# The order of a chunk of the test-time-training scan on four engines, rearranged with the same operations

## The chip, the cores and the metric

One core of a Trainium2 chip runs the whole kernel. The metric is the device time of the execution in microseconds.

## What is computed

The kernel is one transformer block with adaptive layer norm on x of 4x1024x128. Its first half is what the change touches: a small two-layer network is trained by one gradient step for each of the 1024 time steps (on the 4 sequences of the batch), and the trained network is then applied to all tokens. Cut to what matters:

```python
def _mlp(params, h):
    W1, b1, W2, b2 = params
    return silu(h @ W1 + b1) @ W2 + b2
k, v = split(x @ W_KV)                    # time first: (1024, 4, 128) each
def step(params, kvt):
    g = grad(lambda p, k_t, v_t: mean((_mlp(p, k_t) - v_t) ** 2))(params, *kvt)
    return tuple(p - LR * gp for p, gp in zip(params, g)), None
params, _ = scan(step, (W1, b1, W2, b2), (k, v))
out = _mlp(params, x @ W_Q)
```

The second half is a mixture of eight experts with two active and one shared expert. The change leaves it as it is.

## The kernel before

The program is a row of blocks; in each, the engines run their own lists of instructions and meet by semaphores. The scan is one block. It goes through the 1024 steps in 32 chunks of 32 steps, so that a chunk is a tile of 128 columns (32 steps of 4 sequences). Within a chunk the steps depend on each other through the weights; the kernel solves this by iteration. It computes an estimate of the chunk from the weights at its start, with masked gram matrices (`mk`, `mk2`: only earlier steps count) that carry the effect of the steps before, and repeats it with the last estimate.

Three chunks are in work at a time. Chunk n+2 is prepared (names with `q_`: the projection to `kv`, its transpose `kvrow`, its gram matrices `GX`). Chunk n+1 gets a cheap estimate in bf16 (names with `l_` or a final L: `aL`, `eL`, `gL`), before the weights of its start are known exactly. Chunk n gets the f32 iterations (`h_`, a final H: `aH`, `e1H`, `e2H`, `e3H`), and from their result `ge` the weights W1b and W2p are updated. `W2pL` is W2p in bf16, brought forward by the cheap estimate's own sums, with which that of the next chunk is made.

The order is written out by hand. Each of TensorE, ScalarE, VectorE and GpSimd has a function `turn(n, r)` that lists its steps with `do(step, chunk, ring slot)`. Each step is a small function with its waits and one or two instructions. Turns -2 to 3 and 28 to 33 are unrolled, the others stand in a loop of four turns. An engine runs its instructions in the order of its list, and what it waits for holds up all that stands behind.

The steps that matter in what follows, with the lines of the profile:

- TensorE (L389 is the helper `mm`): `h_y_first` (the product aH,W2p) waits for the new W2p; `l_y_first` (W2pL,aL) for the new W2pL; `h_f_last` (W2p,e3H) for e3H; `h_sums1`, `h_sums2` (ge,kvrow and arowH,ge) for ge. `h_gram_a` is the gram product of aH, `h_y_old` a bf16 product with erowL and GaL. `l_turn_q0` (L437) transposes qL.
- VectorE (L770 is the helper `stt`): `l_mask_a1` writes GaL, `h_mask_e2` Ge2H (L845), `h_less1` nH (L853), `l_e_last` eL, `h_slope1` qH from tH and nH, `h_e_last` e3H, `l_mask_e` GeL, `h_g_last` ge, `h_new_W2` W2p, `l_new_W2` W2pL.
- The check of convergence runs beside: GpSimd's `chk_diff` (L993) writes `diff`, the difference between the last two estimates `ge` of a chunk. VectorE's `square` (L773) adds up the squares of `diff` (`chk_add_diff_g`, `chk_add_diff_e`) and of `ge` (`chk_add_norm_g`, `chk_add_norm_e`) into `sums`, each with an instruction that reads the sum out. After the scan these decide whether a slow exact path has to run. It does not with these inputs.
- GpSimd, chunk n+1: `l_less1` nL (L966), `l_more1` oL (L970), `l_slope1` qL (L974); then `q_shift` vb (L946) and `q_lower` GXb (L950).

Of the kernel before, what the change touches and what calls it, by code (L numbers as in the profile page):

```python
# [43 lines left out]
def program(nc, x, w_q, w_kv, w1, b1, w2, b2, w_router,  # L44
            s_w1t, s_b1, s_w2t, s_b2, cond, w_mod, slabs, ident_in, before_in, lower_in, tabs_in, xs, ys, out):
    with ExitStack() as ctx:
# [310 lines left out]
        with block() as blk:  # L357
# [29 lines left out]
            def _(pe):  # L387
# [200 lines left out]
                def turn(n, r):  # L588
                    do(h_gram_a, n, r)
                    do(h_y_old, n, r)  # L590
# [10 lines left out]
                    do(l_turn_q0, n + 1, r + 1)  # L601
                    do(q_turn, n + 2, r + 2)
                    do(h_turn_q0, n, r)
                    do(l_f_first, n + 1, r + 1)
                    do(h_f_add0, n, r)
                    do(h_f_first, n, r)
                    do(l_z_add, n + 1, r + 1)
                    do(l_turn_e2, n + 1, r + 1)
                    do(h_z_new, n, r)
                    do(h_turn_e2, n, r)  # L610
                    do(h_z_last, n, r)
                    do(l_gram_a1, n + 1, r + 1)
                    do(l_turn_a, n + 1, r + 1)
                    do(h_gram_e2, n, r)
# [5 lines left out]
                    do(q_grams, n + 2, r + 2)  # L620
                    do(l_gram_e, n + 1, r + 1)
                    do(h_f_add1, n, r)
                    do(h_turn_q1, n, r)
                    do(h_f_last, n, r)
                    do(l_turn_e, n + 1, r + 1)
                    do(h_turn_e3, n, r)
                    do(l_turn_q1, n + 1, r + 1)
                    do(l_f_second, n + 1, r + 1)
                    do(h_z_base, n + 1, r + 1)
# [6 lines left out]
                    do(l_sums, n + 1, r + 1)  # L636

# [10 lines left out]
            def _(act):  # L648
# [39 lines left out]
                def l_row_e(c, r):  # L688
                    nc.scalar.copy(erowL[1][:, :], LCb[:, 3 * P:4 * P]).then_inc(l_er2, 1)

                def h_act0(c, r):
                    act.wait_ge(h_z, 2 * c + 1)
                    nc.scalar.activation(aH[0][:, :], HZ[:, 0:P], ACT.Silu, bias=W1b[:, (r - 1) % 2, P:P + 1]).then_inc(h_a, 1)  # L693

                def h_tanh0(c, r):
                    nc.scalar.activation(tH[0][:, :], HZ[:, 0:P], ACT.Tanh, bias=b1n[(r - 1) % 2][:, 0:1], scale=-0.5).then_inc(h_t, 1)
# [37 lines left out]
                def turn(n, r):  # L734
                    do(l_act0, n + 1, r + 1)
# [4 lines left out]
                    do(l_row_q0, n + 1, r + 1)  # L740
                    do(h_row_q0, n, r)
                    do(q_rows, n + 2, r + 2)
                    do(l_act1, n + 1, r + 1)
                    do(l_row_e2, n + 1, r + 1)
                    do(h_row_e2, n, r)
# [1041 lines left out]
```

## Time and profile before

| | us |
|---|---|
| median of 3 runs | 749.01 (747.5 to 749.43) |
| the profiled execution, its time | 740.31 |
| its span | 738.5 |
| busy in it: TensorE | 581.0 |
| VectorE | 449.1 |
| GpSimd | 347.2 |
| ScalarE | 322.1 |

The page gives busy times over the whole span. A line of the timeline gives the start of an instruction in us from the span's start, its length, its engine, its line and what it writes and reads. Lengths are from start to result; the next instruction of an engine may start before that. PE stands for TensorE's products, PEld for its weight loads, DVE for VectorE, ACT for ScalarE, POOL for GpSimd. An f32 product of 128 columns is two passes (x2).

### The profile page before, as it was taken

The page shows a single profiled execution, that of the slowest core. Times are in us where ns is not written, and L with a number is a line of the kernel's source. Part 1 is how long each engine was busy: PE and PEld are TensorE (multiplying, and loading weights), DVE is VectorE, ACT ScalarE, POOL GpSimd, SP SyncE. Part 2 cuts the span into 40 slices and gives each one's busy share as a digit, 9 for nine tenths or more (in the row PEclk, how much of TensorE's full clock was granted, in tenths as well). Part 3 has the DMA queues.
Part 4 walks back from the last instruction along what each step waited for, and adds up shares of the span by engine and source line. Part 5 has one row for each costly group of instructions (what it writes and reads, how often), then busy time and mean ns, then how long its engine had stood idle before and what let it go on. Part 6 is the DMA issues. An engine that isn't in the chain of part 4 may idle for free. (4 is left out here: it accounts for less than half of the span.)

```text
span 738.5 us, 14829 instructions
## 1 busy us (share of the span) xinstructions
PE 581.0 (79%) x4319; PEld 520.2 (70%) x4319; DVE 449.1 (61%) x1732; ACT 322.1 (44%) x1022; POOL 347.2 (47%) x558
## 2 busy tenths in 40 slices
PE   1459999999999999997739253003998999999937
PEld 1339999999999999996429252002997999999923
DVE  2847888888888888887286650100995444444505
ACT  1546666666666666663322041000674444434400
POOL 1035666666666666663730077774001555455430
PEclk9999999999999999999775575555899999999969
DMA  9069700000000000000000051111002777777648
GB/s 201 0 273 412 315 2 2 0 0 0 0 0 0 0 0 0 0 1 2 1 1 0 1 204 51 55 51 41 23 1 68 207 228 232 229 232 215 195 143 227
DMA packets 42879, 66.76 MB, mean 90 GB/s; under 512 B 7536, under 2 KB 30832, under 8 KB 42832
## 3 DMA queue, kind: packets, MB, share of 16 engines
q1 hardware_dynamic: 32048, 52.74, 22.8%
q0 software_dynamic: 4544, 9.45, 3.6%
q10 hardware_dynamic: 6240, 4.00, 2.0%
q8 instruction: 22, 0.36, 0.2%
q14 instruction: 25, 0.20, 0.1%
HBM read 36.25 MB, written 29.92 MB: 90 GB/s over the span
## 5 line engine op out<-in xcount | busy, mean ns | idle before, releaser
L1740 POOL DMA_INDIRECT ys<-yo,dst x78 | 74.8, 960 | 128.0 <-DVE yo L1698 112.0
L1621 ACT ACTIVATE hid<-bank,slab 128x256 f32<-128x256 f32 x156 | 63.7, 471 | 81.9 <-PE bank L1550 69.6
L1732 POOL DMA_INDIRECT xs<-hrow,slot_i x64 | 62.6, 979 | 66.6 <-POOLq L1271 47.4
L1561 PEld LDWEIGHTS bank<-slab,hid 128*128 128x128 f32 x624 | 75.6, 192 | 2.0
L1561 PE MATMUL bank<-slab,hid 128*128 128x128 f32 x624 | 75.8, 275 | 0.0
L1550 PE MATMUL bank<-hg,slab 128*128 128x256 f32 x312 | 74.0, 380 | 0.8 <-DVE hg L1674 0.5
L1550 PEld LDWEIGHTS bank<-hg,slab 128*128 128x128 f32 x312 | 56.2, 190 | 7.3 <-issue 0.7
L1533 PE MATMUL bank<-ident,yT 128*128 128x128 f32 x32 | 7.3, 313 | 55.4 <-issue 43.7
L1533 PEld LDWEIGHTS bank<-ident,yT 128*128 128x128 f32 x32 | 4.0, 156 | 57.2 <-issue 44.1
L1606 ACT ACTIVATE hx<-bank,sb 128x256 f32<-128x256 f32 x64 | 26.4, 473 | 40.2 <-remote 31.9
L389 PE MATMUL bank<-aH,W2p 128*128 128x128 f32 x192 | 42.1, 301 | 0.1
L389 PE MATMUL bank<-kv,W1b 128*128 128x128 f32 x192 | 41.2, 297 | 0.0
L1681 DVE SCALAR_TENSOR_TENSOR row<-xt,etab 128x2 f32<-128x2 f32 x39 | 8.6, 221 | 52.1 <-DMA ys<-yo,dst 52.1
L966 POOL TENSOR_TENSOR nL<-aL,ones 128x128 f32<-128x128 bf16 x32 | 17.7, 553 | 41.5 <-ACT aL L675 41.5
L1657 DVE CAST hhH<-hx 128x512 fp32r<-128x512 f32 x32 | 13.5, 423 | 36.8 <-ACT hx L1606 27.3
L978 POOL TENSOR_TENSOR nH<-aH,ones 128x128 f32<-128x128 f32 x32 | 14.6, 456 | 36.7 <-ACT aH L693 36.7
L389 PEld LDWEIGHTS bank<-aH,W2p 128*128 128x128 f32 x192 | 28.9, 190 | 3.3 <-DVE W2p L770 0.3
L1514 PE MATMUL bank<-hgH,w1H 128*128 128x256 f32 x64 | 20.8, 325 | 12.8 <-DVE hgL L1649 9.6
L389 PE MATMUL bank<-GX,ge 128*128 128x128 f32 x128 | 30.7, 322 | 0.1
L1649 DVE TENSOR_TENSOR hgL<-hT,hgH 128x256 fp32r<-128x256 f32 x16 | 6.7, 424 | 39.4 <-issue 37.1
L1613 ACT ACTIVATE yT<-bank,bs2T 128x256 f32<-128x256 f32 x16 | 7.6, 475 | 52.3 <-issue 34.9
L1693 DVE TENSOR_TENSOR yb<-bank,slab 128x256 f32<-128x256 f32 x39 | 16.6, 425 | 22.0 <-PE bank L1561 12.3
(322 smaller groups left out, 2039.1 us busy)
## 6 DMA issues: line engine op xcount, KB each, us to landing
slab<-in_slabs_dram SPq DMA_DIRECT2D x39, 578.0 KB
xs<-fill SPq DMA_DIRECT2D x34, 528.0 KB, 6.1
xt<-xs SPq DMA_DIRECT2D x39, 132.0 KB
xr<-in_L_attn_x_dram SPq DMA_DIRECT2D x8, 256.0 KB, 9.0
yg<-ys SPq DMA_DIRECT2D x4, 512.0 KB, 8.7
yg<-ys ACTq DMA_DIRECT2D x4, 512.0 KB, 9.6
ys<-yo,dst POOLq DMA_INDIRECT x78
xs<-hrow,slot_i POOLq DMA_INDIRECT x64
```

What stands on the lines that cost most here:

```text
L389: return pe.matmul(dst, lhs, rhs, start=start, stop=stop, skip_group_check=True)
L966: pool.tensor_tensor(nL[1][:, :], aL[1][:, :], ones2[:, 0:P], ALU.subtract).then_inc(l_n, 1)
L978: pool.tensor_tensor(nH[0][:, :], aH[0][:, :], ones2[:, 0:P], ALU.subtract).then_inc(h_n, 1)
L1514: mm = pe.matmul(u_half(t, n), w[:, n, :], h[t % 2][:, :], start=(m == 0), stop=(m == 2))
L1550: mm = pe.matmul(e_half(j, n), slab[j % RW][:, n * P:(n + 1) * P], hg[j % 2][:, :], start=True, stop=True)
L1561: mm = pe.matmul(bank[4 + j % 2][:, s * D:(s + 1) * D], hid[j % 2][:, n, s * P:(s + 1) * P], slab[j % RW][:, F + n * P:F + (n + 1) * P], s ...
L1606: nc.scalar.activation(hx[a][:, n % HALF, :], u_half(t, n), ACT.Gelu_apprx_tanh, bias=sb1[:, n:n + 1]).then_inc(x_ready, 1)
L1621: nc.scalar.activation(hid[j % 2][:, n, :], e_half(j, n), ACT.Gelu_apprx_tanh, bias=slab[j % RW][:, 2 * F + n:2 * F + n + 1]).then_inc(e_x, 1)
L1657: dve.tensor_copy(hi, hx[a][:, :, :]).then_inc(hi_ready, 1)
L1693: dve.tensor_tensor(yb[j % 2][:, :, :], bank[4 + j % 2][:, 0:SUB * D].rearrange("p (s d) -> p s d", s=SUB), slab[j % RW][:, 2 * F + FT:SLA ...
L1732: pool.indirect_dma_start(out=xs[:, :], out_offset=bass.IndirectOffsetOnAxis(ap=slot_i[:, c, k:k + 1], axis=0), in_=hrow[:, c, :], in_offs ...
L1740: pool.indirect_dma_start(out=ys[:, :], out_offset=bass.IndirectOffsetOnAxis(ap=dst[r][:, s:s + 1], axis=0), in_=yo[r][:, s, :], in_offset ...
```

## The change

The four lists `turn` are put in another order, and the waits that the new order makes needless or necessary are taken out or put in. No operation is added or taken away. On TensorE some of the bf16 products (`l_` steps and `h_y_old`) are moved next to each other. On ScalarE the tanh for aH comes ahead of its silu. On VectorE and GpSimd the parts of the check of convergence are moved.

```diff
--- before.py
+++ after.py
@@ -586,8 +586,6 @@
                     mm(HU[:, P:2 * P + 1], ge[r % 2][1][:, 1, :], arowH[1][:, :], True, True).then_inc(h_U2, 1)
 
                 def turn(n, r):
-                    do(h_gram_a, n, r)
-                    do(h_y_old, n, r)
                     do(h_y_first, n, r)
                     do(h_turn_a0, n, r)
                     do(l_gram_a0, n + 1, r + 1)
@@ -599,33 +597,33 @@
                     do(l_y_second, n + 1, r + 1)
                     do(h_y_second, n, r)
                     do(l_turn_q0, n + 1, r + 1)
+                    do(h_f_add0, n, r)
+                    do(l_f_first, n + 1, r + 1)
+                    do(l_turn_e2, n + 1, r + 1)
+                    do(h_turn_q0, n, r)
+                    do(h_f_first, n, r)
+                    do(h_turn_e2, n, r)
+                    do(l_z_add, n + 1, r + 1)
                     do(q_turn, n + 2, r + 2)
-                    do(h_turn_q0, n, r)
-                    do(l_f_first, n + 1, r + 1)
-                    do(h_f_add0, n, r)
-                    do(h_f_first, n, r)
-                    do(l_z_add, n + 1, r + 1)
-                    do(l_turn_e2, n + 1, r + 1)
                     do(h_z_new, n, r)
-                    do(h_turn_e2, n, r)
                     do(h_z_last, n, r)
                     do(l_gram_a1, n + 1, r + 1)
+                    do(h_gram_e2, n, r)
                     do(l_turn_a, n + 1, r + 1)
-                    do(h_gram_e2, n, r)
                     do(h_y_lag, n, r)
                     do(l_y_base, n + 1, r + 1)
                     do(l_y_add, n + 1, r + 1)
                     do(h_y_last, n, r)
                     do(h_turn_a1, n, r)
                     do(q_grams, n + 2, r + 2)
+                    do(h_f_add1, n, r)
                     do(l_gram_e, n + 1, r + 1)
-                    do(h_f_add1, n, r)
                     do(h_turn_q1, n, r)
                     do(h_f_last, n, r)
-                    do(l_turn_e, n + 1, r + 1)
                     do(h_turn_e3, n, r)
                     do(l_turn_q1, n + 1, r + 1)
                     do(l_f_second, n + 1, r + 1)
+                    do(l_turn_e, n + 1, r + 1)
                     do(h_z_base, n + 1, r + 1)
                     do(h_sums1, n, r)
                     do(h_z_cross, n + 1, r + 1)
@@ -634,6 +632,8 @@
                     do(l_z_base, n + 2, r + 2)
                     do(l_z_cross, n + 2, r + 2)
                     do(l_sums, n + 1, r + 1)
+                    do(h_y_old, n + 1, r + 1)
+                    do(h_gram_a, n + 1, r + 1)
 
                 pe.wait_ge(cleared, 5)
                 for n in range(-2, RING):
@@ -686,13 +686,14 @@
                     nc.scalar.copy(qrowL[1][:, :], LTb[:, 2 * P:3 * P]).then_inc(l_qr, 1)
 
                 def l_row_e(c, r):
+                    act.wait_ge(l_T2, 2 * c + 2)
                     nc.scalar.copy(erowL[1][:, :], LCb[:, 3 * P:4 * P]).then_inc(l_er2, 1)
 
                 def h_act0(c, r):
+                    nc.scalar.activation(aH[0][:, :], HZ[:, 0:P], ACT.Silu, bias=W1b[:, (r - 1) % 2, P:P + 1]).then_inc(h_a, 1)
+
+                def h_tanh0(c, r):
                     act.wait_ge(h_z, 2 * c + 1)
-                    nc.scalar.activation(aH[0][:, :], HZ[:, 0:P], ACT.Silu, bias=W1b[:, (r - 1) % 2, P:P + 1]).then_inc(h_a, 1)
-
-                def h_tanh0(c, r):
                     nc.scalar.activation(tH[0][:, :], HZ[:, 0:P], ACT.Tanh, bias=b1n[(r - 1) % 2][:, 0:1], scale=-0.5).then_inc(h_t, 1)
 
                 def h_row_e1(c, r):
@@ -732,28 +733,28 @@
                     nc.scalar.copy(ge[r % 2][1][:, 1, :], HY[:, P:2 * P]).then_inc(h_er2, 1)
 
                 def turn(n, r):
-                    do(l_act0, n + 1, r + 1)
                     do(l_tanh0, n + 1, r + 1)
                     do(h_row_a0, n, r)
                     do(h_row_e1, n, r)
                     do(q_copy, n + 2, r + 2)
                     do(l_row_q0, n + 1, r + 1)
+                    do(l_row_e2, n + 1, r + 1)
                     do(h_row_q0, n, r)
+                    do(l_act1, n + 1, r + 1)
+                    do(h_row_e2, n, r)
                     do(q_rows, n + 2, r + 2)
-                    do(l_act1, n + 1, r + 1)
-                    do(l_row_e2, n + 1, r + 1)
-                    do(h_row_e2, n, r)
                     do(h_act1, n, r)
                     do(h_tanh1, n, r)
                     do(l_tanh1, n + 1, r + 1)
+                    do(l_row_a, n + 1, r + 1)
                     do(h_row_a1, n, r)
-                    do(l_row_a, n + 1, r + 1)
                     do(h_row_q1, n, r)
+                    do(h_row_e3, n, r)
                     do(l_row_q1, n + 1, r + 1)
-                    do(h_row_e3, n, r)
                     do(l_row_e, n + 1, r + 1)
+                    do(h_tanh0, n + 1, r + 1)
                     do(h_act0, n + 1, r + 1)
-                    do(h_tanh0, n + 1, r + 1)
+                    do(l_act0, n + 2, r + 2)
 
                 nc.scalar.preload_act_table_set("silu_and_others")
                 for n in range(-2, RING):
@@ -782,6 +783,7 @@
                     dve.tensor_tensor(e1rowL[:, :], LC[:, 0:P], vb[r][:, :], ALU.subtract).then_inc(l_e, 1)
 
                 def l_mask_a0(c, r):
+                    dve.wait_ge(l_gram, 3 * c + 1)
                     stt(GaL[0][:, :], LG[:, 0:P], 1.0, mk[:, :], ALU.add, ALU.mult).then_inc(l_Ga, 1)
 
                 def l_e_second(c, r):
@@ -860,7 +862,6 @@
                 def h_g_last(c, r):
                     dve.wait_ge(h_qr, 2 * c + 2)
                     dve.wait_ge(h_f, 2 * c + 2)
-                    after(dve, chk_norm_g, c - 1)
                     stt(ge[r % 2][1][:, 0, :], qrowH[1][:, :], 2.0, HG[:, 2 * P:3 * P], ALU.add, ALU.mult).then_inc(h_g, 1)
 
                 def h_new_W1(c, r):
@@ -877,10 +878,10 @@
                     stt(W2p[:, :], HU[:, 0:2 * P + 1], -KAPPA, W2p[:, :], ALU.mult, ALU.add).then_inc(h_W2, 1)
 
                 def chk_add_diff_g(c, r):
+                    dve.wait_ge(chk_d, c + 1)
                     square(0, diff[:, 0, :]).then_inc(chk_diff_g, 1)
 
                 def chk_add_diff_e(c, r):
-                    dve.wait_ge(chk_d, c + 1)
                     square(2, diff[:, 1, :]).then_inc(chk_diff_e, 1)
 
                 def chk_add_norm_g(c, r):
@@ -895,28 +896,28 @@
                     do(l_new_W2, n, r)
                     do(h_mask_a, n, r)
                     do(h_e_first, n, r)
+                    do(l_mask_a0, n + 1, r + 1)
                     do(l_e_first, n + 1, r + 1)
                     do(l_new_b2, n, r)
-                    do(l_mask_a0, n + 1, r + 1)
                     do(h_mask_e1, n, r)
                     do(l_e_second, n + 1, r + 1)
                     do(h_e_second, n, r)
                     do(l_g_first, n + 1, r + 1)
-                    do(chk_add_norm_g, n - 2, r - 2)
+                    do(chk_add_diff_e, n - 2, r - 2)
                     do(h_g_first, n, r)
+                    do(chk_add_norm_g, n - 1, r - 1)
+                    do(l_mask_a1, n + 1, r + 1)
                     do(chk_add_norm_e, n - 1, r - 1)
-                    do(chk_add_diff_e, n - 1, r - 1)
-                    do(l_mask_a1, n + 1, r + 1)
+                    do(h_less1, n, r)
                     do(h_mask_e2, n, r)
-                    do(h_less1, n, r)
                     do(l_e_last, n + 1, r + 1)
                     do(h_slope1, n, r)
                     do(h_e_last, n, r)
+                    do(chk_add_diff_g, n - 1, r - 1)
                     do(l_mask_e, n + 1, r + 1)
+                    do(h_g_last, n, r)
                     do(q_mask, n + 2, r + 2)
-                    do(h_g_last, n, r)
                     do(l_g_last, n + 1, r + 1)
-                    do(chk_add_diff_g, n - 1, r - 1)
                     do(h_new_W1, n, r)
                     do(h_new_b1, n, r)
                     do(h_new_W2, n, r)
@@ -986,20 +987,18 @@
                     pool.tensor_tensor(qH[0][:, :], nH[0][:, :], oH[:, :], ALU.mult).then_inc(h_q0, 1)
 
                 def chk_diff(c, r):
-                    pool.wait_ge(h_g, 2 * c + 2)
-                    pool.wait_ge(h_er2, 2 * c + 2)
                     after(pool, chk_diff_g, c)
                     after(pool, chk_diff_e, c)
                     pool.tensor_tensor(diff[:, :, :], ge[r % 2][1][:, :, :], ge[r % 2][0][:, :, :], ALU.subtract).then_inc(chk_d, 1)
 
                 def turn(n, r):
-                    do(h_more0, n, r)
                     do(l_less0, n + 1, r + 1)
                     do(l_more0, n + 1, r + 1)
                     do(l_slope0, n + 1, r + 1)
+                    do(h_more0, n, r)
                     do(h_slope0, n, r)
+                    do(l_less1, n + 1, r + 1)
                     do(chk_diff, n - 1, r - 1)
-                    do(l_less1, n + 1, r + 1)
                     do(l_more1, n + 1, r + 1)
                     do(l_slope1, n + 1, r + 1)
                     do(q_shift, n + 2, r + 2)
```

Two places of the order as the program holds it. The first is VectorE, from the product's error e2H (chunk n) to the error e3H. `junk,sums<-ge,sums` and `junk,sums<-diff,sums` are the squares, `sums 128x1` their read-outs. Before:

```order
L773 ISA junk,sums<-ge,sums 128x128
L773 ISA sums 128x1
L773 ISA junk,sums<-diff,sums 128x128
L773 ISA sums 128x1
L770 SCALAR_TENSOR_TENSOR GaL<-bank,mk 128x128
L845 TENSOR_TENSOR Ge2H<-bank,mk 128x128
L853 TENSOR_SCALAR nH<-aH 128x128
L802 REGISTER_ALU
L770 SCALAR_TENSOR_TENSOR eL<-bank,b2L,kv 128x128
L770 SCALAR_TENSOR_TENSOR qH<-tH,nH 128x128
L770 SCALAR_TENSOR_TENSOR e3H<-bank,W2p,kv 128x128
```

With the change:

```order
L771 SCALAR_TENSOR_TENSOR GaL<-bank,mk 128x128
L774 ISA junk,sums<-ge,sums 128x128
L774 ISA sums 128x1
L855 TENSOR_SCALAR nH<-aH 128x128
L847 TENSOR_TENSOR Ge2H<-bank,mk 128x128
L804 REGISTER_ALU
L771 SCALAR_TENSOR_TENSOR eL<-bank,b2L,kv 128x128
L771 SCALAR_TENSOR_TENSOR qH<-tH,nH 128x128
L771 SCALAR_TENSOR_TENSOR e3H<-bank,W2p,kv 128x128
L774 ISA junk,sums<-diff,sums 128x128
```

One square of ge now stands behind GaL and one of diff behind e3H; nH and Ge2H have changed places.

The second is GpSimd, chunks n and n+1. Before:

```order
L954 TENSOR_TENSOR nL<-aL,ones 128x128
L958 TENSOR_TENSOR oL<-tL,ones 128x128
L961 ISA
L962 TENSOR_TENSOR qL<-nL,oL 128x128
L985 REGISTER_ALU
L986 TENSOR_TENSOR qH<-nH,oH 128x128
L989 ISA
L993 TENSOR_TENSOR diff<-ge 128x256
L965 REGISTER_ALU
L966 TENSOR_TENSOR nL<-aL,ones 128x128
L970 TENSOR_TENSOR oL<-tL,ones 128x128
```

With the change:

```order
L959 TENSOR_TENSOR oL<-tL,ones 128x128
L962 ISA
L963 TENSOR_TENSOR qL<-nL,oL 128x128
L982 ISA
L983 TENSOR_TENSOR oH<-tH,ones 128x128
L986 REGISTER_ALU
L987 TENSOR_TENSOR qH<-nH,oH 128x128
L966 REGISTER_ALU
L967 TENSOR_TENSOR nL<-aL,ones 128x128
L369 REGISTER_ALU
L992 TENSOR_TENSOR diff<-ge 128x256
L971 TENSOR_TENSOR oL<-tL,ones 128x128
```

`diff` has moved from ahead of the second nL (`l_less1`) to between it and oL, and oH from the turn's start to behind the first qL.

## Rows read from the trace of the kernel before

**Rows 1.** The page, part 1: busy us, share of the span, instructions.

```profile
PE 581.0 (79%) x4319; PEld 520.2 (70%) x4319; DVE 449.1 (61%) x1732; ACT 322.1 (44%) x1022; POOL 347.2 (47%) x558
```

**Rows 2.** Busy us by stretch, one stretch of the scan: PE, PEld, DVE, ACT, POOL, clock.

```profile
150.00:200.00 50.00, 50.00 (x442) 45.70 (x441) 41.34 (x177) 31.64 (x121) 31.27 (x64) 1.00 0.00 0
```

**Rows 3.** Timeline, PE: start us, length us, engine, line, out<-in; L437 twice.

```profile
150.09 0.22 PE L437 MATMUL bank<-identb,qL 128*128 128x128 bf16 x1
...
159.26 0.22 PE L437 MATMUL bank<-identb,qL 128*128 128x128 bf16 x1
```

**Rows 4.** Timeline, DVE, one turn.

```profile
151.07 0.34 DVE L773 CUSTOM_DVE_ANT_0 junk<-ge,sums 128x128 f32<-128x128 f32 x1
151.35 0.08 DVE L773 DVE_READ_ACCUMULATOR2_ANT sums<- 128x1 f32 x1
151.38 0.29 DVE L770 SCALAR_TENSOR_TENSOR ge<-qrowH,bank 128x128 f32<-128x128 f32 x1
...
151.86 0.35 DVE L773 CUSTOM_DVE_ANT_0 junk<-diff,sums 128x128 f32<-128x128 f32 x1
...
152.31 0.29 DVE L770 SCALAR_TENSOR_TENSOR GaL<-bank,mk 128x128 bf16<-128x128 f32 x1
152.64 0.29 DVE L845 TENSOR_TENSOR Ge2H<-bank,mk 128x128 f32<-128x128 f32 x1
152.85 0.22 DVE L853 TENSOR_SCALAR nH<-aH 128x128 f32<-128x128 f32 x1
152.98 0.35 DVE L770 SCALAR_TENSOR_TENSOR eL<-bank,b2L,kv 128x128 bf16<-128x128 f32 x1
153.25 0.57 DVE L770 SCALAR_TENSOR_TENSOR qH<-tH,nH 128x128 f32<-128x128 f32 x1
153.74 0.34 DVE L770 SCALAR_TENSOR_TENSOR e3H<-bank,W2p,kv 128x128 f32<-128x128 f32 x1
```

**Rows 5.** Timeline, weight loads (PEld) and DVE, links of the chain behind e3H.

```profile
154.13 0.30 PEld L389 LDWEIGHTS bank<-W2p,e3H 128*128 128x128 f32 x2
...
156.66 0.43 DVE L770 SCALAR_TENSOR_TENSOR W2p<-bank,W2p 128x257 f32<-128x257 f32 x1 [0.47 <-PE bank L389]
...
157.66 0.10 PEld L389 LDWEIGHTS bank<-W2pL,aL 128*128 128x128 bf16 x1
```

**Rows 6.** Timeline, PEld: two f32 passes, then a group of bf16 products.

```profile
156.27 0.30 PEld L389 LDWEIGHTS bank<-kv,W1b 128*128 128x128 f32 x2
156.50 0.10 PEld L389 LDWEIGHTS bank<-GXb,gL 128*128 128x128 bf16 x1
156.61 0.10 PEld L389 LDWEIGHTS bank<-erowL,arowL 128*128 128x128 bf16 x1
156.66 0.10 PEld L389 LDWEIGHTS bank<-arowL,erowL 128*128 128x128 bf16 x1
```

**Rows 7.** Timeline, POOL, the same turn.

```profile
151.93 0.57 POOL L966 TENSOR_TENSOR nL<-aL,ones 128x128 f32<-128x128 bf16 x1 [1.26 <-ACT aL L675]
153.22 0.45 POOL L970 TENSOR_TENSOR oL<-tL,ones 128x128 f32<-128x128 f32 x1 [0.72 <-ACT tL L678]
153.75 0.46 POOL L974 TENSOR_TENSOR qL<-nL,oL 128x128 bf16<-128x128 f32 x1
154.17 0.46 POOL L946 TENSOR_TENSOR vb<-kvrow,tabs 128x128 f32<-128x128 f32 x1
...
159.10 0.73 POOL L993 TENSOR_TENSOR diff<-ge 128x256 f32<-128x256 f32 x1
```

**Rows 8.** Timeline, DVE and POOL, where the last chunks are left.

```profile
335.07 0.61 DVE L773 CUSTOM_DVE_ANT_0 junk<-diff,sums 128x128 f32<-128x128 f32 x1
...
335.11 0.43 POOL L966 TENSOR_TENSOR nL<-aL,ones 128x128 f32<-128x128 bf16 x1 [1.05 <-ACT aL L675]
...
345.17 0.29 DVE L770 SCALAR_TENSOR_TENSOR qH<-tH,nH 128x128 f32<-128x128 f32 x1
345.39 0.35 DVE L770 SCALAR_TENSOR_TENSOR e3H<-bank,W2p,kv 128x128 f32<-128x128 f32 x1
```

More of the change, by code:

```diff
@@ L688, in l_row_e @@
                 def l_row_e(c, r):
+                    act.wait_ge(l_T2, 2 * c + 2)
                     nc.scalar.copy(erowL[1][:, :], LCb[:, 3 * P:4 * P]).then_inc(l_er2, 1)
                 def h_act0(c, r):
-                    act.wait_ge(h_z, 2 * c + 1)
                     nc.scalar.activation(aH[0][:, :], HZ[:, 0:P], ACT.Silu, bias=W1b[:, (r - 1) % 2, P:P + 1]).then_inc(h_a, 1)
                 def h_tanh0(c, r):
+                    act.wait_ge(h_z, 2 * c + 1)
                     nc.scalar.activation(tH[0][:, :], HZ[:, 0:P], ACT.Tanh, bias=b1n[(r - 1) % 2][:, 0:1], scale=-0.5).then_inc(h_t, 1)
```

## Prediction

> **What bounds the kernel now.** I read the page first: TensorE is busy for 581.0 us, 79% of the span [rows 1]. That is a mean over stages with different limits. The change touches the scan alone, so next come the busy times by stretch. In a stretch of the scan TensorE counts as busy for all 50.00 us and its clock is granted in full, 2.4 GHz [rows 2]. That looks like a kernel bound by TensorE, but its ends are modelled, so the third view is the order of time within one chunk. A chunk repeats every 9.17 us (the transpose of qL at L437 starts at 150.09 and again at 159.26) [rows 3]. Set against it what a turn's products need if nothing waits. By the starts of the weight loads two f32 passes take 0.22 us, so 0.11 each; a bf16 product behind an f32 one takes 0.11, the next 0.05 [rows 6]. A turn has 25 f32 products of two passes and 9 f32 transposes, so 59 f32 passes, and 22 bf16 products in 13 groups: 59x0.11 + 22x0.055 + 13x0.055 = 8.4 us. The remaining 0.8 us TensorE waits, in short pieces. So the turn is a closed chain in which TensorE, VectorE and ScalarE relieve each other, and what comes late on VectorE in such a place makes the whole turn late.
>
> The important link of the chain: VectorE writes e3H from 153.74 to 154.08 [rows 4], and TensorE loads the weights of the product with it (h_f_last) at 154.13, which is 0.05 later. Behind that stand, by the code, ge, the sums, W2p and W2pL, each waiting for the one ahead: W2p is written from 156.66 to 157.09, and TensorE loads W2pL at 157.66 for the chunk that comes next [rows 5]. I see no slack between these links, and take a delay of e3H to be paid in full, once a turn.
>
> **The change, part by part.**
>
> 1. *bf16 products closer together.* In a group of bf16 products the first one holds TensorE for 0.11 us and the next for 0.05 [rows 6]. The new order joins h_y_old and l_turn_e to other groups and parts l_turn_a from l_gram_a1: 12 groups where there were 13. That is 0.055 us a turn, 32x0.055 = 1.8 us at most. But h_y_old now stands just ahead of the wait for W2p. What TensorE saves there it waits longer: 0 on the path.
>
> 2. *Transposes pulled into waits* (q_turn behind l_z_add, h_turn_q0 and h_turn_e2 ahead of it). They fill time in which TensorE waits for e2H and gL. The end of those waits is set by VectorE, which keeps its order there: 0. If TensorE's own row decided instead, the gain would be bounded by all its waits, 0.8 us a turn.
>
> 3. *ScalarE: tanh before silu for aH, and l_act0 at the turn's end.* aH is written some 0.27 us later. Behind it stand h_gram_a, now ahead of the wait for W2p, and GpSimd's nH, and with h_more0 moved back GpSimd's qH comes about 0.4 us later. TensorE needs that qH behind the product with e2L. No row here shows how much room is left: I take 0, since that product still waits for VectorE, with a bound of 0.4 us a turn if all of it came through.
>
> 4. *Waits.* Those removed (h_act0, chk_diff, h_g_last) are for events that an earlier instruction of the engine has seen. Those added (l_mask_a0, l_row_e, chk_add_diff_g) stand where the event is long past. 0.
>
> 5. *VectorE's squares of the check.* Today the squares of norm_e and diff_e (0.27 us each from start to start) are done before l_mask_a1, in time in which VectorE would wait for TensorE's gram product anyway: the second starts at 151.86 and lets the engine go 0.31 later, and GaL starts only at 152.31 [rows 4]. The change moves one square (norm_e) **behind** GaL, ahead of nH, and another (diff_g) to behind e3H, where it can only delay GeL. Today: GaL 152.31, a wait, Ge2H 152.64, nH 152.85, eL 152.98, qH 153.25, e3H 153.74. Afterwards, with the same distances: GaL 152.31, square 152.52, its read-out 152.79, nH 152.82, Ge2H 152.95, eL 153.16, qH 153.43. qH starts 0.18 late.
>
> 6. *GpSimd: chk_diff is moved to behind l_less1.* Here the trace shows something that the order does not. In the last chunk, with GpSimd silent, qH took 0.29 us; in all the others, starting 0.03 us after GpSimd's oL, it takes 0.57, as at 153.25 beside oL's 153.22 [rows 4, 7, 8]. And one square took 0.61 instead of 0.35, beside a GpSimd nL that started 0.04 us after it [rows 8]. So a VectorE operation with two sources in SBUF waits for a GpSimd operation under way: 0.28 us longer beside oL, so until 0.31 us after oL's start, which is 0.15 before its end; 0.26 longer beside nL, so until 0.20 before nL's end. The other way round, nL takes 0.57 in place of 0.43 when the square is 0.07 ahead [rows 4, 7, 8].
>    The Trainium skill ("SBUF — State Buffer", "Who interferes with whom") says that a VectorE instruction with two SBUF inputs and a GpSimd instruction that reads SBUF take turns at a shared port, the first to come keeping it for its whole length; the trace agrees. By a reading of the order alone, without it, the sum would be part 5's 5.6 us.
>    Now chk_diff, 0.73 us long [rows 7], stands behind nL. nL, no longer delayed, goes from 151.93 to 152.36, and diff from 152.31 to 153.04. The square that would start at 152.52 gets its turn at 152.84 to 152.89. Then nH at 153.15 to 153.20, and qH, 0.61 later, at 153.76 to 153.81. GpSimd's qL starts at 153.75 [rows 7], at the same time or just before. qH then waits until 153.75 + 0.31 = 154.06, and e3H starts 0.22 later (qH's distance when alone [rows 8]) at 154.28. Today it is 153.74: **0.54 us late per turn**.
>
> Sum: 0.54 us in the 31 turns that have a chunk behind them to check: 16.7 us. The profiled execution, 740.31 us, would become 757.0. The median of the three runs, 749.01, stands 1.2% above it; I add the same amount to that: 765.7.
>
> **Rivals.**
>
> *A second collision at nH.* oL starts at 153.22 [rows 7], and nH would start at 153.15 to 153.20. If nH too has to take turns with GpSimd and loses, it waits until 153.53; qH comes at 154.14, beside vb at 154.17, and is either just ahead (e3H at 154.36, 0.62 late) or waits again to 154.48 (e3H at 154.70, 0.96 late). 31 turns: 19 to 30 us, 768 to 779. For it: near ties of this kind were lost at 0.04 us ahead and won at 0.07. Against: nH has one source only, and no row shows one such beside GpSimd. The skill (same page and section) has a rule that speaks for this rival: a tensor_scalar from SBUF to SBUF can use both ports and then contends as well. No row of this trace decides it.
>
> *The first collision alone.* If qH is ahead of qL, e3H starts at 153.78 + 0.22 = 154.00, 0.26 late: 8 us, 757. It needs oL delayed by nH by 0.1 us.
>
> *No collisions.* If the square gets through beside diff, part 5 is left: 0.18 us, 5.6 us, 754.6. It would need the 0.61 us square to have another cause.
>
> *The cover holds.* If the delay ends in slack that I do not see (the ge wait also hangs on ScalarE's qrowH), it is no change: 749.
>
> *Faster.* TensorE's row of products is the bound, as its 50.00 of 50.00 says. Then the saved group (1.8 us) and what is filled of the waits (at most 0.8 us a turn, 26 us) count, and VectorE's delay is hidden. I take 3 us, near the lower end, since only two of the waits get other work: 746. It decides from the point where e3H's product no longer starts 0.05 us behind e3H; today it does, each turn. Against it speaks also that this order leaves the work behind e3H as it was.
>
> **How the numbers follow.** The forecast of 765.7 gets 0.36, the second collision 0.20, the first alone 0.13, none 0.13, the cover 0.08, faster 0.10. The first four are slower: 0.82. A measurement here tells 0.3% (2.2 us) from no change. The range takes in the cases from no collision to the worse second collision, 754 to 779, and leaves out the last two. The likeliest case's own range is 762 to 768.
>
> **What would show it.** In the trace of the changed kernel: the turn 9.7 us long rather than 9.17; the square behind GaL 0.6 to 0.7 us long rather than 0.35, beside diff; nH 0.3 us later after GaL than now; qH 0.5 us or more again, beside qL and no longer beside oL; W2p,e3H still 0.05 us behind e3H. If nH takes 0.5 us rather than 0.22, it is the second collision. If the square takes 0.35 us, part 6 is wrong; if TensorE does not wait for e3H, the whole argument is.

## The result, and the profile after

| | before | changed |
|---|---|---|
| median of 20 runs each (lowest to highest) | 746.46 (742.24 to 749.85) | 752.08 (748.24 to 754.62) |
| span of the profiled execution | 738.5 | 751.5 |
| length of a turn in the scan | 9.17 | 9.35 |

The changed kernel is slower: ratio 1.0075, 95% interval 1.0055 to 1.0095, so 5.6 us. The forecast had the sign, but 16.7 us, and the result lies below its range of 754 to 779. Part of that is the basis: the forecast started from a median of three runs, 749.01, and the twenty give 746.46. On the old basis 5.6 us would make 754.6, just inside. The size is wrong on either basis, and that is what has to be explained.

The page gives the busy times; columns as in [rows 1]:

```profile
PE 586.1 (78%) x4319; PEld 524.9 (70%) x4319; DVE 445.8 (59%) x1732; ACT 322.5 (43%) x1022; POOL 351.1 (47%) x558
```

The stretch of [rows 2] in the changed kernel:

```profile
150.00:200.00 50.00, 50.00 (x436) 45.70 (x434) 39.63 (x170) 30.52 (x117) 32.65 (x66) 1.00 0.00 0
```

TensorE's 50.00 of 50.00 and the granted clock of 1.00 are as before, and yet fewer products fit in: 436 for 442. The full busy share hides the waits, as the prediction said.

The page's groups already show what moved. Columns: line, engine, operation, count, busy us, mean ns, idle time before them. `...` stands here and below for lines left out.

```profile
L967 POOL TENSOR_TENSOR nL<-aL,ones 128x128 f32<-128x128 bf16 x32 | 13.7, 428 | 47.5 <-ACT aL L675 47.5
...
L774 DVE CUSTOM_DVE_ANT_0 junk<-ge,sums 128x128 f32<-128x128 f32 x64 | 32.3, 507 | 0.0
```

GpSimd's nL takes 428 ns for 553 before: no square stands beside it now. The squares of ge take 507 ns on average: half of them 340, the other half 670.

The timeline of one turn, VectorE, as in [rows 4]:

```profile
201.70 0.29 DVE L771 SCALAR_TENSOR_TENSOR GaL<-bank,mk 128x128 bf16<-128x128 f32 x1 [0.36 <-PE bank L389]
201.91 0.67 DVE L774 CUSTOM_DVE_ANT_0 junk<-ge,sums 128x128 f32<-128x128 f32 x1
202.51 0.08 DVE L774 DVE_READ_ACCUMULATOR2_ANT sums<- 128x1 f32 x1
202.51 0.22 DVE L855 TENSOR_SCALAR nH<-aH 128x128 f32<-128x128 f32 x1
202.65 0.28 DVE L847 TENSOR_TENSOR Ge2H<-bank,mk 128x128 f32<-128x128 f32 x1
202.85 0.33 DVE L771 SCALAR_TENSOR_TENSOR eL<-bank,b2L,kv 128x128 bf16<-128x128 f32 x1
203.10 0.28 DVE L771 SCALAR_TENSOR_TENSOR qH<-tH,nH 128x128 f32<-128x128 f32 x1
203.30 0.34 DVE L771 SCALAR_TENSOR_TENSOR e3H<-bank,W2p,kv 128x128 f32<-128x128 f32 x1
```

GpSimd in the same turn, as in [rows 7]:

```profile
201.32 0.43 POOL L967 TENSOR_TENSOR nL<-aL,ones 128x128 f32<-128x128 bf16 x1 [1.47 <-ACT aL L675]
201.71 0.73 POOL L992 TENSOR_TENSOR diff<-ge 128x256 f32<-128x256 f32 x1
202.61 0.46 POOL L971 TENSOR_TENSOR oL<-tL,ones 128x128 f32<-128x128 f32 x1 [0.17 <-ACT tL L678]
203.14 0.56 POOL L975 TENSOR_TENSOR qL<-nL,oL 128x128 bf16<-128x128 f32 x1
```

And TensorE behind it, weight loads, as in [rows 5], with W2p and W2pL on VectorE below:

```profile
203.69 0.30 PEld L389 LDWEIGHTS bank<-W2p,e3H 128*128 128x128 f32 x2
```

```profile
206.23 0.43 DVE L771 SCALAR_TENSOR_TENSOR W2p<-bank,W2p 128x257 f32<-128x257 f32 x1 [0.47 <-PE bank L389]
206.84 0.42 DVE L771 SCALAR_TENSOR_TENSOR W2pL<-bank,W2p 128x256 bf16<-128x256 f32 x1 [0.18 <-DVE W2p L771]
```

Read it in time from GaL. Before, GaL's start to e3H's was 1.43 us (152.31 to 153.74); now it is 1.60 (201.70 to 203.30). The square behind GaL takes 0.67, beside a diff that started 0.20 ahead of it, where it would take 0.34: 0.33 lost. But qH takes 0.28 in place of 0.57: it starts 0.49 behind oL now, no longer 0.03, and 0.04 **ahead** of qL, which is the one that waits (0.56 for 0.46). Two instructions that take turns in this way I call a collision; one came here and another went. Behind e3H all is as it was: the load of its product 0.05 behind its end.

To compare turns of different kernels I count below from the start of L437's weight load, as the median of the scan's turns. In these terms e3H starts at 3.76 before and at 3.93 in the changed kernel, qL at 3.76 in both. Such medians are good to 0.01 us.

### The profile page after: what moved, and what is told of

The parts are those of the page before. It is cut to its first block and busy times, and to the rows that moved or that the text cites. A ratio compares the mean times of both kernels' runs of the same rounds, so it can differ in the third digit from the quotient of the medians.

```text
span 751.5 us, 14803 instructions
## 1 busy us (share of the span) xinstructions
PE 586.1 (78%) x4319; PEld 524.9 (70%) x4319; DVE 445.8 (59%) x1732; ACT 322.5 (43%) x1022; POOL 351.1 (47%) x558
## 5 line engine op out<-in xcount | busy, mean ns | idle before, releaser
L967 POOL TENSOR_TENSOR nL<-aL,ones 128x128 f32<-128x128 bf16 x32 | 13.7, 428 | 47.5 <-ACT aL L675 47.5
L951 POOL TENSOR_TENSOR GXb<-GX,ones 128x256 bf16<-128x256 f32 x32 | 23.3, 727 | 25.0 <-DVE GX L771 25.0
L774 DVE CUSTOM_DVE_ANT_0 junk<-ge,sums 128x128 f32<-128x128 f32 x64 | 32.3, 507 | 0.0
L389 PEld LDWEIGHTS bank<-kv,W1b 128*128 128x128 f32 x192 | 29.8, 196 | 0.2
```

What stands on the lines that cost most here:

```text
L389: return pe.matmul(dst, lhs, rhs, start=start, stop=stop, skip_group_check=True)
L774: return dve.tensor_tensor_reduce(junk[:, k, :], src, src, 1.0, sums[:, k:k + 1], ALU.mult, ALU.add, sums[:, k:k + 1])
L951: pool.tensor_tensor(GXb[r][:, :, :].rearrange("p k t -> p (k t)"), GX[r][:, :, :].rearrange("p k t -> p (k t)"), ones2[:, :], ALU.mult).t ...
```

## The experiments

**Theory A**: the squares, qH and perhaps nH take turns with GpSimd; per turn the changed kernel pays 0.33 for square beside diff and 0.18 for the square's new place, and gets back what qH paid beside oL. **Theory B**: the place of the square alone costs its own 0.18, which over 31 turns is 5.6 us, exactly what was measured. **Theory C**: the new order on TensorE and ScalarE costs it. Each kernel was timed together with the kernel before, whose median lay between 742.97 and 746.11 from group to group, so the ratio to it is what counts.

*pool_back.* GpSimd's list as before, with the two waits of `chk_diff`, all else changed:

```diff
+                    pool.wait_ge(h_g, 2 * c + 2)
+                    pool.wait_ge(h_er2, 2 * c + 2)
...
+                    do(h_more0, n, r)
                     do(l_less0, n + 1, r + 1)
                     do(l_more0, n + 1, r + 1)
                     do(l_slope0, n + 1, r + 1)
-                    do(h_more0, n, r)
                     do(h_slope0, n, r)
+                    do(chk_diff, n - 1, r - 1)
                     do(l_less1, n + 1, r + 1)
-                    do(chk_diff, n - 1, r - 1)
```

> The changed kernel, but GpSimd's list is that of before: chk_diff ahead of l_less1 again, with its two waits, and h_more0 at the turn's start. VectorE, TensorE and ScalarE keep the changed order, so the square of norm_e still stands behind GaL. Theory A (the two squares and qH take turns with GpSimd; the changed kernel pays 0.33 us a turn for the square beside diff and gains 0.28 because qH no longer stands beside oL): here no diff is under way at the square, so it takes 0.34 us and not 0.67; qH starts about 3.40 to 3.45 us after L437, behind oL again, and waits for it, so e3H starts where it did in the kernel before (3.76): ratio 1.000, within 0.002. Theory B (the place of the square alone costs its own 0.18 us a turn, collisions don't reach the end): ratio as in the changed kernel, 1.0075. Theory C (the new order on TensorE and ScalarE costs the time): also 1.0075.

Measured: 743.98 against 742.97, ratio 1.0017 (0.9998 to 1.0037). The square behind GaL takes 0.34, e3H starts at 3.76. The *other* square of ge now starts together with diff and takes longer still:

```profile
198.33 0.88 DVE L774 CUSTOM_DVE_ANT_0 junk<-ge,sums 128x128 f32<-128x128 f32 x1
199.14 0.08 DVE L774 DVE_READ_ACCUMULATOR2_ANT sums<- 128x1 f32 x1
199.14 0.28 DVE L771 SCALAR_TENSOR_TENSOR GaL<-bank,mk 128x128 bf16<-128x128 f32 x1
```

```profile
198.33 0.73 POOL L994 TENSOR_TENSOR diff<-ge 128x256 f32<-128x256 f32 x1 [1.37 <-DVE sums L774]
```

That one sits in the wait for GaL's product, so 0.54 of stall make GaL only 0.10 late, and qH's own wait behind oL (0.35 for qH) swallows that.

*small_diff.* Nothing is moved. GpSimd's diff is made short, and a memset at the start clears the rest of `diff`, so the kernel leaves out most of the check's sum:

```diff
-                    pool.tensor_tensor(diff[:, :, :], ge[r % 2][1][:, :, :], ge[r % 2][0][:, :, :], ALU.subtract).then_inc(chk_d, 1)
+                    pool.tensor_tensor(diff[:, :, 0:8], ge[r % 2][1][:, :, 0:8], ge[r % 2][0][:, :, 0:8], ALU.subtract).then_inc(chk_d, 1)
...
+                nc.gpsimd.memset(diff[:, :, :], 0.0)
```

> The changed kernel, with every instruction in its changed place, but GpSimd's diff works on 8 of the 128 columns (the rest of diff is set to zero once at the start): the check of convergence then leaves out the other columns. Theory A: diff is over before the square of norm_e starts, which takes 0.34 us; qH starts at 3.40 to 3.45 us after L437, and is behind oL (3.23) again, so it takes 0.4 us or more, and e3H starts at about 3.76 in place of 3.93: ratio 1.000 to 1.001. Theory B (place of the square alone, 0.18 us a turn): no change against the changed kernel, 1.0075. The forecast's own part 6 without its qL term would give the same as A here.

Measured: 743.01 against 742.97, ratio 1.0008 (0.9994 to 1.0022). The timeline, VectorE:

```profile
199.80 0.34 DVE L774 CUSTOM_DVE_ANT_0 junk<-ge,sums 128x128 f32<-128x128 f32 x1
...
200.66 0.44 DVE L771 SCALAR_TENSOR_TENSOR qH<-tH,nH 128x128 f32<-128x128 f32 x1
201.03 0.34 DVE L771 SCALAR_TENSOR_TENSOR e3H<-bank,W2p,kv 128x128 f32<-128x128 f32 x1
```

and GpSimd:

```profile
199.59 0.22 POOL L992 TENSOR_TENSOR diff<-ge 128x16 f32<-128x16 f32 x1
200.50 0.46 POOL L971 TENSOR_TENSOR oL<-tL,ones 128x128 f32<-128x128 f32 x1 [0.68 <-ACT tL L678]
```

Theories B and C fall: every instruction stands in its changed place, and the time is that of before. Up to the square nothing else differs from the changed kernel: GaL starts at 2.32 and the square at 2.53 in both, and so do oL at 3.23 and qL at 3.76. It also shows why the place alone costs nothing. qH starts 0.13 later than before, but behind oL it would have waited anyway, and its end stays 0.60 after oL's start. The changed kernel's account per turn is then 0.33 for the wait of the square and 0.13 for its place, less the 0.29 of qH's wait: 0.17, as e3H is late. The agreement of 5.6 us with theory B was chance.

*norm_first.* One step back, chk_add_norm_e ahead of l_mask_a1:

```diff
-                    do(l_mask_a1, n + 1, r + 1)
                     do(chk_add_norm_e, n - 1, r - 1)
+                    do(l_mask_a1, n + 1, r + 1)
```

> The changed kernel with one step moved back: VectorE's chk_add_norm_e stands ahead of l_mask_a1 again. GpSimd's diff stays behind l_less1. Theory A: the square is over before GaL and before diff starts; nH follows GaL as soon as aH is there (about 2.70 us after L437), qH comes at about 3.29 us, behind oL's 3.23, and waits for it; e3H at 3.76 as before the change: ratio 1.000, within 0.002. Theory B (place alone) expects the same, 1.000, so this run tells both from theory C (TensorE and ScalarE's order): 1.0075.

Measured: 746.93 against 742.97, ratio 1.0067 (1.0043 to 1.0091). I missed this one. VectorE:

```profile
200.74 0.29 DVE L771 SCALAR_TENSOR_TENSOR GaL<-bank,mk 128x128 bf16<-128x128 f32 x1
201.08 0.61 DVE L855 TENSOR_SCALAR nH<-aH 128x128 f32<-128x128 f32 x1
201.61 0.28 DVE L847 TENSOR_TENSOR Ge2H<-bank,mk 128x128 f32<-128x128 f32 x1
```

and GpSimd:

```profile
200.88 0.72 POOL L992 TENSOR_TENSOR diff<-ge 128x256 f32<-128x256 f32 x1
```

With the square gone, **nH** stands beside diff and takes 0.61 for 0.22. The prediction's rival of a second collision at nH had this doubt against it, that nH has one source only. The doubt was wrong; e3H comes at 3.86, and the turn takes 9.29. The Trainium skill ("SBUF — State Buffer", "Who interferes with whom") has the rule that a tensor_scalar from SBUF to SBUF can take both ports and then contends with GpSimd. This row agrees that it contends.

*pad_qH and pad128_qH.* These were meant to turn the near tie of qH and qL, by an extra instruction ahead of qH in the changed kernel, a memset of 64 or of 128 columns of an unused tile `pad`. The first:

```diff
                     dve.wait_ge(h_t, 2 * c + 2)
+                    dve.memset(pad[:, 0:64], 0.0)
                     stt(qH[1][:, :], tH[1][:, :], 1.0, nH[1][:, :], ALU.add, ALU.mult).then_inc(h_q1, 1)
```

> The changed kernel with one small extra VectorE instruction right ahead of qH: a memset of 64 columns of an unused tile, 0.06 to 0.14 us. It moves qH from 0.04 us ahead of GpSimd's qL (3.73 against 3.77 us after L437) to 0.02 to 0.10 us behind it. Theory A: qH now loses its turn to qL and takes about 0.55 us in place of 0.28; e3H starts at about 4.28 in place of 3.93, and the turn is 0.35 us longer: 31 times that is 10.8 us above the changed kernel, ratio 1.022. Theory B (no collision reaches the end): only the extra instruction counts, 0.06 to 0.14 us a turn, 2 to 4 us, ratio 1.010 to 1.013.

> As pad_qH, with a memset of 128 columns. The runs so far say that what counts is where qH would end if alone: it gets through when that is 0.24 to 0.26 us after qL's start (changed kernel 4.00 against 3.77, pad_qH 4.03 against 3.77) and waits when it is 0.30 after oL's start (kernel before, 3.26 + 0.28 against 3.23). The memset of 64 columns put its end back by 0.02 us only; one of 128 takes about 0.07 more, so the end alone would be 4.09, 0.33 after qL's start. Theory A: qH now loses, its end goes to 4.35 and e3H's start to 4.28; ratio 1.022 (31 times 0.35 us more than the changed kernel). Theory B (collisions don't reach the end): e3H 0.1 later than in the changed kernel, ratio 1.012.

Measured: ratio 1.0112 (1.0089 to 1.0135) and 1.0089 (1.0062 to 1.0117), turns of 9.37 and 9.44. Neither turned it: theory A's expectation of 1.022 was missed twice, and pad_qH's ratio is what was expected without a lost tie. In pad128_qH, VectorE and then GpSimd:

```profile
223.32 0.17 DVE L861 MEMSET pad<- 128x128 f32 x1
223.41 0.22 DVE L772 SCALAR_TENSOR_TENSOR qH<-tH,nH 128x128 f32<-128x128 f32 x1
223.55 0.33 DVE L772 SCALAR_TENSOR_TENSOR e3H<-bank,W2p,kv 128x128 f32<-128x128 f32 x1
```

```profile
223.30 0.64 POOL L977 TENSOR_TENSOR qL<-nL,oL 128x128 bf16<-128x128 f32 x1
```

qL takes 0.64 and ends 0.31 after qH's end, much as in the changed kernel (0.32, 203.70 after 203.38). It looks as if the memset itself takes the turn and hands it to qH. That wasn't tried by itself, and these two runs say nothing for or against a lost tie. The next one needed an extra instruction that reads no SBUF.

*extra_eL.* In the changed kernel:

```diff
                     dve.wait_ge(l_y, 3 * c + 3)
+                    dve.tensor_copy(pad[:, 0:8], LC[:, 0:8])
                     stt(eL[:, :], LC[:, 0:P], b2L[:, 0:1], kv[r][:, P:2 * P], ALU.add, ALU.subtract).then_inc(l_e, 1)
```

> The changed kernel with one small extra VectorE instruction ahead of eL: a copy of 8 columns from eL's PSUM bank to an unused tile. Unlike the memsets of pad_qH and pad128_qH, behind which qL was held back 0.12 and 0.19 us and never came first, this one writes little to SBUF and reads none. It puts qH back by about 0.13 us, to 3.86 us after L437, 0.1 behind qL's start of 3.77. Theory A: qL now has its turn first and takes 0.46 us; qH's start when it gets through is 3.77 + 0.33 = 4.10 (0.33: qH's wait behind oL in pe_act, whose end is 3.83, 0.60 after oL's start), e3H at about 4.29 in place of 3.93: 0.36 us a turn, ratio 1.022. Theory B (no collision with qL reaches the end): e3H 0.13 later than in the changed kernel, ratio 1.013.

Measured: 758.1 against 743.07, ratio 1.0207 (1.0171 to 1.0244). VectorE:

```profile
206.10 0.15 DVE L806 COPY pad<-bank 128x8 f32<-128x8 f32 x1
206.17 0.34 DVE L772 SCALAR_TENSOR_TENSOR eL<-bank,b2L,kv 128x128 bf16<-128x128 f32 x1
206.43 0.56 DVE L772 SCALAR_TENSOR_TENSOR qH<-tH,nH 128x128 f32<-128x128 f32 x1
206.92 0.34 DVE L772 SCALAR_TENSOR_TENSOR e3H<-bank,W2p,kv 128x128 f32<-128x128 f32 x1
```

GpSimd:

```profile
206.39 0.46 POOL L977 TENSOR_TENSOR qL<-nL,oL 128x128 bf16<-128x128 f32 x1
```

An instruction that moves its successors by 0.07 us costs 0.37 us a turn (9.72 for 9.35). qH starts 0.04 behind qL and not 0.04 ahead, and now it is qH that waits. e3H starts at 4.29, 0.53 later than in the kernel before.

That is so in 24 turns. In six others of the same kernel qH got through, in five of them although it started 0.03 behind qL, as here, VectorE and then GpSimd:

```profile
294.16 0.28 DVE L772 SCALAR_TENSOR_TENSOR qH<-tH,nH 128x128 f32<-128x128 f32 x1
```

```profile
294.13 0.62 POOL L977 TENSOR_TENSOR qL<-nL,oL 128x128 bf16<-128x128 f32 x1
```

The three such turns within the loop's regular part are only 0.07 to 0.09 longer than the same turns of the changed kernel. So of the 0.37 the extra instruction itself costs less than 0.1, and the lost tie the rest.

*pe_act and dve_pool.* The two halves of the change: TensorE's and ScalarE's lists changed, the others as before, and the reverse.

```diff
                     do(l_turn_q0, n + 1, r + 1)
+                    do(h_f_add0, n, r)
+                    do(l_f_first, n + 1, r + 1)
+                    do(l_turn_e2, n + 1, r + 1)
+                    do(h_turn_q0, n, r)
...
```

That is the start of TensorE's part, which pe_act has and dve_pool lacks; the others likewise.

> TensorE's and ScalarE's lists of the changed kernel (bf16 products closer together, transposes in waits, tanh first) with VectorE's and GpSimd's lists of before. Theory A, and the forecast's parts 1 to 4: nothing, since e3H is written at the same time: 1.000, within 0.002. Rival (TensorE's row of products decides): 0.998 or less, 1.8 us for the saved group and more for filled waits.

> VectorE's and GpSimd's lists of the changed kernel with TensorE's and ScalarE's of before; the complement of pe_act. Theory A: the whole loss is here, since pe_act had none: ratio 1.0075, if the events reach VectorE and GpSimd at the same times. ScalarE writes aH earlier and TensorE takes qL's transposes in the old order, so oL or qL may fall elsewhere against qH, which by theory A can add up to 0.3 us a turn: up to 1.018. If the lists only cost together: 1.000.

Measured: pe_act 0.9999 (0.9972 to 1.0026), dve_pool 1.0155 (1.0124 to 1.0185). So the parts do not add up to 1.0075: TensorE's and ScalarE's new order is worth nothing alone, and 0.16 us a turn (9.51 against 9.35) beside the new lists of the others. In dve_pool gL comes 0.16 late. TensorE's row there shows what waits:

```profile
201.77 0.27 PE L398 MATMUL bank<-ident,kv 128*128 128x128 f32 x1
202.04 0.33 PE L525 MATMUL bank<-ident,qH 128*128 128x128 f32 x1
202.20 0.22 PE L389 MATMUL bank<-W2pL,e2L 128*128 128x128 bf16 x1
```

GpSimd's qH comes later, since `h_more0` was moved back:

```profile
201.52 0.46 POOL L986 TENSOR_TENSOR qH<-nH,oH 128x128 f32<-128x128 f32 x1
```

and the product with e2L, for which gL waits, is queued behind its transpose. The changed TensorE order has that product ahead of it.

*dve_pool_q0.* That one step, in dve_pool:

```diff
                     do(q_turn, n + 2, r + 2)
-                    do(h_turn_q0, n, r)
                     do(l_f_first, n + 1, r + 1)
                     do(h_f_add0, n, r)
+                    do(h_turn_q0, n, r)
                     do(h_f_first, n, r)
```

> dve_pool with one step of TensorE moved: h_turn_q0, which waits for GpSimd's qH, stands behind l_f_first and h_f_add0 and no longer ahead of them. In dve_pool it waits 0.15 us for qH (transposed 0.44 us after L437's start, in the kernel before 0.29), and gL comes 0.15 us later than in the changed kernel (1.04 against 0.88 us after L437's load). Theory A: that wait is what dve_pool pays above the changed kernel, and what TensorE's new order spares. Now gL is back at 0.88; part of the gain may be lost where qH's own transpose comes later. Ratio between 1.0075 and 1.014. If the wait for qH has nothing to do with it (ScalarE's order instead): gL stays at 1.04, ratio 1.0155.

Measured: 1.0128 (1.0094 to 1.0162), which the interval does not tell from dve_pool. gL is back at 0.88, so its wait was qH's. But the turn is shorter by 0.01 only: qH is now transposed at 0.88, in the changed kernel at 0.66. In the changed kernel the product arowH,Ge1H (`h_f_add0`) is done ahead of the product with e2L. dve_pool_q0 has q_turn's transposes of kv in that place, and `h_f_add0` stands between the product with e2L and qH's transpose. So ge, which needs qH's transpose, starts at 1.49 in place of 1.40, and GaL at 2.43 in place of 2.32. The one step moves the delay; it takes more of the new order to lose it. Which steps are enough wasn't tried, nor ScalarE's order by itself.

*qH_first and qH_first_plus.* If a collision at qH costs time, the kernel before can be made faster, for it pays one in each turn. qH_first is the kernel before with this one step moved. qH_first_plus is pe_act with the same move and two more, q_mask behind e3H and, on TensorE, qH's transpose ahead of the product with eL:

```diff
                     do(h_less1, n, r)
+                    do(h_slope1, n, r)
                     do(l_e_last, n + 1, r + 1)
-                    do(h_slope1, n, r)
                     do(h_e_last, n, r)
```

> The kernel before with one step moved: VectorE's h_slope1 (qH) stands ahead of l_e_last (eL), so right behind nH. Theory A: qH starts at about 3.0 us after L437, ahead of GpSimd's oL (3.23), and takes 0.28 us in place of 0.57; eL starts at 3.20 and e3H at 3.46 in place of 3.76. That is 0.3 us; but eL is 0.2 us later, and on TensorE the gram product with eL stands ahead of h_turn_q1 and h_f_last, so part of it may be kept back there: between 0.05 and 0.3 us a turn, ratio 0.988 to 0.998. If the collision did not matter to the end: 1.000 or, by the later eL, above.

> pe_act with three steps moved: VectorE's h_slope1 ahead of l_e_last and q_mask behind h_e_last, and TensorE's h_turn_q1 behind h_f_add1, ahead of the gram product with eL. Theory A: qH is transposed and e3H's product loaded without waiting for eL, so more of the 0.3 us comes through than in qH_first: 0.1 to 0.3 us a turn, ratio 0.988 to 0.996. If the collision did not matter: 1.000.

Measured: 0.9967 (0.9942 to 0.9991) and 0.9958 (0.9936 to 0.9980); the second is 743.48 against 746.11. VectorE in qH_first_plus:

```profile
199.45 0.29 DVE L771 SCALAR_TENSOR_TENSOR qH<-tH,nH 128x128 f32<-128x128 f32 x1
199.66 0.34 DVE L771 SCALAR_TENSOR_TENSOR eL<-bank,b2L,kv 128x128 bf16<-128x128 f32 x1
199.92 0.34 DVE L771 SCALAR_TENSOR_TENSOR e3H<-bank,W2p,kv 128x128 f32<-128x128 f32 x1
```

GpSimd's oL starts behind qH:

```profile
199.62 0.46 POOL L971 TENSOR_TENSOR oL<-tL,ones 128x128 f32<-128x128 f32 x1 [0.72 <-ACT tL L678]
```

The collision is gone, and this version beats both kernels. But e3H starts 0.23 earlier (3.53 for 3.76), and the turn is only 0.10 shorter; in qH_first 0.17 earlier and 0.05 shorter. Late, e3H is paid in full; early, less than half comes back. Some 0.09 of it is lost at once, on TensorE:

```profile
200.40 0.30 PEld L389 LDWEIGHTS bank<-W2p,e3H 128*128 128x128 f32 x2
```

That is 0.14 behind e3H's end at 200.26, and no longer 0.05; in qH_first it is 0.15. Where the rest of the gain goes wasn't traced.

*qH_first_W2.* One more step moved, in qH_first_plus:

```diff
                     do(l_g_last, n + 1, r + 1)
+                    do(h_new_W2, n, r)
                     do(chk_add_diff_g, n - 1, r - 1)
                     do(h_new_W1, n, r)
                     do(h_new_b1, n, r)
-                    do(h_new_W2, n, r)
```

> qH_first_plus with one more step moved: VectorE's h_new_W2 (W2p) ahead of chk_add_diff_g, h_new_W1 and h_new_b1's place kept otherwise, so that the square and W1b cannot stand between gL and W2p. Theory A: e3H's gain is kept back on TensorE, between e3H's product and the sums that W2p waits for, so VectorE's order here brings little: 0 to 0.05 us a turn against qH_first_plus, ratio 0.994 to 0.996. If VectorE kept W2p back: 0.992 or less.

Measured: 776.58 against 743.07, ratio 1.0441 (1.0409 to 1.0474), a plain mistake of mine. W2p still starts at 6.57, when its sums are there, but W1b, which could go at 5.61, now queues behind it until 7.24. TensorE's product with W1b waits for it, and the turn is 10.24 us:

```profile
220.84 0.28 DVE L771 SCALAR_TENSOR_TENSOR W1b<-bank,W1b 128x129 f32<-128x129 f32 x1
...
221.18 0.49 PE L389 MATMUL bank<-kv,W1b 128*128 128x128 f32 x2 [1.11 <-DVE W1b L771]
```

## Why the prediction was wrong in size

- *Parts 1 to 4, TensorE, ScalarE, waits: 0.* Right: pe_act has TensorE's and ScalarE's order alone (0.9999), and small_diff has all of it (1.0008). But part 3's remark that qH of GpSimd comes later and that no row shows how much room is left was the right worry: with TensorE's and ScalarE's old order it costs 0.16 us a turn (dve_pool), and the new one spares it. Parts 2 and 3 belonged together.
- *Part 5, the square behind GaL: 0.18 late.* The move is as told, but the price is none by itself: small_diff has it and is at 1.0008, since qH stood behind oL anyway. The sum took the place of a square as lost time without asking whether the wait behind it would take it up.
- *Part 6, the square beside diff.* Right: it takes 0.67, and its read-out starts at 3.13, which is 153.11 on the forecast's scale, the early end of what 152.84 to 152.89 for the square's turn give.
- *Part 6, qH beside qL.* **This is the step that failed**: "GpSimd's qL starts at 153.75 [rows 7], at the same time or just before. qH then waits". The forecast had qH at 153.76 to 153.81. On the same scale it came at 153.71: nH started together with the read-out, at 153.11, and not 0.03 behind it, and nH to qH was 0.60 and not 0.61. That is 0.05 to 0.10 sooner, and enough to be 0.04 ahead of qL, so that qL waited (0.56 for 0.46) and qH took 0.28. The sum took a near tie, decided by a few hundredths of a microsecond, as a loss. Its measure of a tie was off as well: it held that 0.04 ahead is lost and 0.07 ahead won, and qH won at 0.04. extra_eL sets qH just behind qL and gives what the forecast priced: e3H 0.53 late for 0.54, and 15.0 us where 16.7 stood, six turns being won. So mechanism and price were right, and the case did not occur.
- *The rival of the first collision alone* is what happened, with e3H 0.17 late and not 0.26, and 5.6 us for 8. The condition set for it, that oL be delayed by nH, was not needed: oL took 0.46.
- *The second collision at nH* did not occur in the changed kernel, where nH starts 0.10 ahead of oL. That nH can collide is shown by norm_first.
- *No collisions* has 5.6 us too, which is what was measured, but by chance: the square did wait, 0.67 for 0.34.
- *The cover holds* and *faster* fall: a late e3H came through in full, and the new order of TensorE and ScalarE gained nothing (pe_act).
- *The chain behind e3H has no slack*: right for a delay (0.17 late, turn 0.18 longer; 0.53 and 0.55), wrong for a gain (0.23 early, 0.10 shorter).

Of the profiled executions' 13 us, the scan has 6.45: its last ge starts at 346.58 before and at 353.03 in the changed kernel. The rest lies behind it, outside the part that the change touches, in single executions of kernels whose runs spread over 6 to 8 us; I give no cause for it.

## What to carry to other kernels

When VectorE and GpSimd both work out of SBUF, an order is not a list of lengths: write beside each VectorE instruction which GpSimd instruction it meets. A delay can be swallowed by a meeting that was being paid for already, or turn a tie and cost five times its size. Price a near tie as two cases with like chances, and test it by moving one instruction by less than 0.1 us. And search the kernel as it is for a meeting that it pays in each turn: taking qH from beside oL gave 0.3% by one moved step (0.9967, interval 0.9942 to 0.9991).

## What the runs showed that I had not expected

- **Who comes first shows better in the end than in the start.** A square that started 0.04 ahead of nL lost [rows 8], a qH 0.04 ahead of qL got through. By the ends it fits: a qH that got through ended 0.24 us after qL's start (changed kernel), and one that lost would have ended, at its 0.28 alone, 0.31 after oL's start (kernel before) or 0.31 to 0.32 after qL's (extra_eL). But at 0.31 it goes both ways: the qH at 294.16 in extra_eL got through there, while others at the same distance lost. The displayed times, good to 0.01, do not decide such a tie. A qH that lost ended 0.60 after the GpSimd instruction's start in each case (before, small_diff, extra_eL), and a square beside diff 0.87 to 0.88 after diff's start (changed kernel, pool_back).
- **A one-source operation takes turns too**: nH 0.61 beside diff in norm_first, 0.22 in the kernel before and in the changed one.
- **Behind a memset qH kept its turn** in pad128_qH, though it started 0.11 after qL and ended 0.33 after qL's start, which the rule above would call lost; the GpSimd instruction waited 0.18.
- **Halves that don't add up**: pe_act costs nothing, dve_pool 1.55%, and both together 0.75%.
